# One table of places for all engines' orders, down projection and embedding in four parts, one transfer per broadcast row

## Chip, cores and metric

One core of a Trainium2 chip runs one program. The metric is the device time of one execution in microseconds; the median of three runs stands for the kernel. TensorE is PE, VectorE DVE, ScalarE ACT, GpSimd POOL; SyncE, SP, issues the transfers.

## What is computed

A one-layer model over 64 images with text. Each image's 196 patches of 768 numbers are normalized and projected to 192 (`D`), 128 text rows are appended (324 rows, `L`), then two residual blocks follow.

```python
h = concat([layernorm(patches) @ W + b + pos, txt], axis=1)       # 64 x 324 x 192
x = layernorm(h)
B_, C_ = split(x @ W_bc.T + b_bc)                                  # 16 numbers each (N)
delta = softplus((x @ W_1.T + b_1) @ W_d.T + b_d)                  # 64 x 324 x 192
# for each of 16 states n, along the 324 rows i:
#   s[i] = exp(delta[i] * A[n]) * s[i-1] + delta[i] * B_[i, n] * x[i];   y[i] += s[i] * C_[i, n]
h = h + y
x = layernorm(h)
# 128 experts, the best 6 for each row by sigmoid(x @ Wg.T) + e_bias, weights normalized, times 2.5,
# capacity 192 rows an expert; routed = sum of w * (silu(x @ G) * (x @ U)) @ Dn
shared = (silu(x @ Wsg) * (x @ Wsu)) @ Wsd                         # 928 hidden
h = h + routed + shared
```

## The kernel before

The work is in two stages. `phase1` takes the images in 32 pairs and does everything but the routed experts; `phase2` then runs over the 128 experts (gather rows, two projections, scatter-add). The change is in `phase1` alone.

In `phase1` 192 channels of two images are laid on 128 partitions as three blocks of 324 (`[128, 3, L]`, 972 numbers a partition): 128 channels of the one image, 128 of the other, and the remaining 64 of both, one on each half of the partitions. For each of 16 states `n` there are: `fill_b` (SP loads the row of B into `b_wide[n % 2]`; POOL multiplies it with `du` into `state[n % 4]`), `decay` (ACT, exp into one of two PSUM areas), `scan` (DVE, the recurrence), `load_c` and `fill_c` (SP loads C's row; DVE multiplies; POOL adds to `y`). B, C and the step-size row are small results of PE (`bc_values`) that SP stores to `dram_bc` by six transfers and that are then read back, repeated over partitions: `dram_bc` has 2 x 2 x 16 rows (parity of the pair, half, state) of 9 x 324 numbers (B, C, step size). In `fill_b`, `load_c` and `load_s` each half of the partitions, 64, is filled by a transfer of its own from its own row (L437, L443, L461).

The rest of a pair: `load_x`, `emb_a` and `emb` (patch projection and the sums of squares, PE, into the bank `sums`), `emb_stats`, `emb_scale`; `ln1_stats`, `ln1_apply`, `x1_turn` (transposes), `bc_values`, `step_size`, `softplus` (gives `delta` and `du`, semaphore `du_ready`); after the scans `resid`, `ln2_stats`, `ln2_apply`, `x2_turn`, `gate`, `choose`, `weigh`, `count`; then the shared expert as sixteen pieces `up_g` k (PE two matmuls, ACT tanh into `th`, DVE `ag`) and sixteen `up_u` k (PE two matmuls, DVE product into `inter`), with two PSUM areas taken in turn, and three blocks of `down_a` and `down` (8 matmuls for each of two images, PE, into `sums`; DVE adds), and `store_out`.

All five engines' orders are written out by hand. `schedule(engine)` gives every piece a step on each engine that it uses, 32 steps a body; a piece has a lag, the number of bodies after its pair's scans (negative: before). A body runs all pieces sorted by step, each for the pair that its lag says. `run_bodies` writes the first and last bodies out and makes a loop of two bodies a turn of the 26 in the middle. An engine runs its list strictly in order, and waits on semaphores in front of a piece; so a wait holds up all that stands behind it. Pieces that share the PSUM banks `work` and `sums` count their uses (`use_number`) for these waits. SP is such a list as well: a transfer that has to wait for its buffer holds up the transfers behind it. The experts' loads are `w_up` (96 rows) and `w_down` (116 rows of 3,072 B, L944).

Of the kernel before, what the change touches and what calls it, by code (L numbers as in the profile page):

```python
# [15 lines left out]
PATCH, PC = 768, 6  # L16
# [39 lines left out]

def schedule(engine):
    at = []  # L60

    def put(piece, lag, k, **steps):
        if engine in steps:
            at.append((steps[engine], len(at), (piece, lag, k)))

    for n in range(N):

        b, lag = 2 * n - 4, 0
        if b < 0:
            b, lag = b + 32, -1  # L70
        put("fill_b", lag, n, sp=b, pool=b + 3)
        c, lag = 2 * n - 2.3, 0
        if c < 0:
            c, lag = c + 32, -1
        put("load_c", lag, n, sp=c)
        d, lag = (2 * n - 1.5, 0) if n else (30.5, -1)
        put("decay", lag, n, act=d + 0.3)
        put("scan", 0, n, dve=2 * n)
        put("fill_c", 0, n, dve=2 * n + 1.2, pool=2 * n + 2)
    for k in range(3):  # L80
        put("down_a", 3, k, pe=0.1 + 2 * k)
        put("down", 3, k, pe=1.1 + 2 * k, dve=2.1 + 2 * k)
        put("store_out", 3, k, sp=3.6 + 2 * k)
        put("resid", 1, k, pe=4.9 + 1.8 * k, dve=5.7 + 1.8 * k)
        put("x2_turn", 1, k, pe=15.2 + 1.1 * k, act=16.2 + 1.1 * k)
        put("x1_turn", -1, k, pe=18.2 + 1.1 * k, act=19.2 + 1.1 * k)
    put("load_x", -2, 0, sp=1.5)
    put("load_txt", -1, 0, sp=10.2)
    put("ln2_stats", 1, 0, dve=10.3, act=11.3)
    put("ln2_apply", 1, 0, dve=12.3, act=13)  # L90
    put("emb_scale", -1, 0, dve=11.1)
    put("ln1_stats", -1, 0, dve=12.4, act=13.4)
    put("ln1_apply", -1, 0, dve=14.4, act=15.4)
    for k in range(2):
        put("gate", 1, k, pe=22.1 + k, act=23.3 + k)
        put("emb_a", -2, k, pe=8.5 + 6 * k, act=7.5 + 5.2 * k)
        put("emb", -2, k, pe=9.5 + 5.85 * k, act=13.2 + 5.85 * k)
    put("bc_values", -1, 0, pe=21.5, act=22.3, sp=22.9)
    put("load_s", -1, 0, sp=24.1)
    for k in range(2):  # L100
        put("step_size", -1, k, act=26.2 + k)
    put("softplus", -1, 0, act=28.5, dve=29.2)
    for k in range(3):
        put("choose", 2, k, dve=1.3 + k)
    put("weigh", 2, 0, dve=5)
    put("weigh", 2, 1, dve=6)
    put("count", 2, 0, pe=3.2, dve=5.2)
    put("store_mid", 2, 0, sp=6.5)
    put("find_a", 2, 0, dve=7.5)
    put("find", 2, 0, pe=7.6, dve=8.6)  # L110
    put("emb_stats", -2, 0, dve=20.4, act=21.4)
    for k in range(2 * NJ):
        for n, piece in enumerate(("up_g", "up_u")):
            step = 6.6 + 0.8 * (2 * (k // 2 * 2 + n) + k % 2)
            put(piece, 2, k, pe=step, act=step + 0.6, dve=step + 0.8)
    return [piece for _, _, piece in sorted(at)]


SCHEDULE = {engine: schedule(engine) for engine in ("pe", "act", "dve", "pool", "sp")}

# [3 lines left out]
FIRST_BODY, LOOP_FROM, LOOP_TO, LAST_BODY = -2, 3, 29, PAIRS + 2  # L124
# [7 lines left out]
def bank_uses(i):  # L132

    return [sum(BANK.get(kind) == bank for kind, _, _ in pieces("pe", i)) for bank in (WORK, SUMS)]


def use_number(i, before):


    def use(piece, k, ago=0):  # L140
        bank = BANK[piece]
        same = [(x[0], x[2]) for x in pieces("pe", i - ago) if BANK.get(x[0]) == bank]
        return before[bank] - (len(same) if ago else 0) + same.index((piece, k)) + 1
    return use


def run_bodies(eng, engine, body):

    before = [0, 0]
    add = lambda n, times: [b + x * times for b, x in zip(before, n)]  # L150
    for i in range(FIRST_BODY, LOOP_FROM):
        body(Turn.fixed(i), pieces(engine, i), use_number(i, before))
        before = add(bank_uses(i), 1)
    steady = bank_uses(LOOP_FROM)
    with eng.Fori(0, (LOOP_TO - LOOP_FROM) // 2) as r:
        for q in range(2):
            start = Turn.fixed(LOOP_FROM + q)
            so_far = [x + 2 * n * r for x, n in zip(add(steady, q), steady)]
            body(Turn(start.v + 2 * r, start.p, start.h + r), pieces(engine, LOOP_FROM), use_number(LOOP_FROM, so_far))
    before = add(steady, LOOP_TO - LOOP_FROM)  # L160
    for i in range(LOOP_TO, LAST_BODY + 1):
        body(Turn.fixed(i), pieces(engine, i), use_number(i, before))
        before = add(bank_uses(i), 1)
# [200 lines left out]
def phase1(nc, ctx, a, out, dram_x, dram_cnt, dram_bc, ident, found):  # L364
# [54 lines left out]
    def bc_rows(t, half, first, rows):  # L419

        at = (2 * t.p + half) * N + first
        return dram_bc[at:at + rows]

    with nc.Block() as block:

        @block.sync
        def _(sp):
            def body(i, todo, use):
                for kind, lag, k in todo:
                    t = i.plus(-lag)  # L430
                    if kind == "fill_b":
# [4 lines left out]
                        for half in range(2):  # L436
                            sp.dma_start(b.b_wide[k % 2][HI * half:HI * half + HI].rearrange("p a t -> p (a t)"),  # L437
                                         bc_rows(t, half, k, 1)[:, 0:3 * L].broadcast_to([HI, 3 * L])).then_inc(b_loaded[k % 2], 16)
                    elif kind == "load_c":

                        wait(sp, c_used, N * t.v + k - 1)
                        for half in range(2):
                            sp.dma_start(b.c_wide[k % 2][HI * half:HI * half + HI].rearrange("p a t -> p (a t)"),  # L443
                                         bc_rows(t, half, k, 1)[:, 3 * L:6 * L].broadcast_to([HI, 3 * L])).then_inc(c_loaded[k % 2], 16)
                    elif kind == "bc_values":

                        sp.wait_ge(work_free, use(kind, k))
                        wait(sp, c_used, N * (t.v - 1))
                        for image in range(2):
                            rows = b.bcv[N * image:N * image + N]  # L450
                            for half in range(2):
                                to = bc_rows(t, half, 0, N).rearrange("n (c q t) -> n c q t", c=3, q=3)
                                sp.dma_start(to[:, :, image, :], rows).then_inc(bc_stored, 16)
                                if half == image:
                                    sp.dma_start(to[:, :, 2, :], rows).then_inc(bc_stored, 16)
                    elif kind == "load_s":
# [12 lines left out]
                    elif kind == "store_out":  # L469
                        sp.wait_ge(sums_free, use("down", k))  # L470
# [17 lines left out]
        def _(pool):  # L488
            def body(i, todo, use):
                for kind, lag, n in todo:  # L490
                    t = i.plus(-lag)
                    if kind == "fill_b":
# [3 lines left out]
                        pool.wait_ge(b_loaded[n % 2], 32 * (N // 2 * t.v + n // 2 + 1))  # L496
# [16 lines left out]
        def _(act):  # L513
# [7 lines left out]
            def body(i, todo, use):  # L521
                for kind, lag, k in todo:
# [9 lines left out]
                    elif kind == "emb_a":  # L532
# [608 lines left out]
```

## Time and profile before

| | us |
|---|---|
| median of 3 runs (5800.55 to 5816.44) | 5815.71 |
| profiled execution | 5808.81 |
| its span, first to last instruction | 5806.8 |
| PE busy | 4271.5 (74%) |
| DVE busy | 3764.1 (65%) |
| POOL busy | 3097.6 (53%) |
| ACT busy | 2051.7 (35%) |
| mean granted TensorE clock | 0.838 |
| DMA, mean over the span | 144 GB/s |

"Busy" is the time in which an engine has an instruction under way; the DMA share is the mean busy share of sixteen DMA engines. A stretch that is named by two times is counted from the span's start. "Landing" is the time from a transfer's issue to its semaphore.

### The profile page before, as it was taken

What the parts mean: (1) busy time and instruction counts of PE and PEld (TensorE: products, weight loads), DVE (VectorE), ACT (ScalarE), POOL (GpSimd) and SP (SyncE); (2) the same over time, 40 slices, a digit from 0 to 9 for tenths busy, and PEclk for the clock granted to TensorE, in tenths of its full rate; (3) what the DMA queues carried; (4) which work ended last, traced back from release to release, by engine and by line L of the source; (5) the groups of instructions that cost most, each with busy time, mean ns of one, the idle gap of its engine ahead of it and who ended that gap; (6) DMA issues with size and microseconds to landing.
All of it is one profiled execution on the core that took longest, in us unless ns stands there. A gap on an engine that the chain in (4) does not pass through costs nothing. (4 is left out here: it accounts for less than half of the span.)

```text
span 5806.8 us, 71026 instructions
## 1 busy us (share of the span) xinstructions
PE 4271.5 (74%) x19964; PEld 3364.6 (58%) x19964; DVE 3764.1 (65%) x6446; ACT 2051.7 (35%) x3874; POOL 3097.6 (53%) x1769
## 2 busy tenths in 40 slices
PE   3357777777777777777777777777788788778877
PEld 2335555555555555555555555545677777777777
DVE  2778777778878778777777877786333333333333
ACT  2544454444445444454444445543111111111110
POOL 0765555555556555555555555653255555555554
PEclk7578878888878888878888888889888888888888
DMA  3776666666666666666666666663255555555554
GB/s 89 187 170 172 159 149 156 163 153 166 159 149 161 160 161 157 157 149 156 165 159 157 159 150 161 169 156 90 73 126 126 128 123 128 125 120 128 128 126 105
DMA packets 331418, 837.85 MB, mean 144 GB/s; under 512 B 59152, under 2 KB 143572, under 8 KB 331208
## 3 DMA queue, kind: packets, MB, share of 16 engines
q1 hardware_dynamic: 279928, 764.79, 52.7%
q0 software_dynamic: 49152, 69.84, 6.6%
q10 hardware_dynamic: 2128, 1.26, 0.1%
q14 instruction: 182, 1.49, 0.1%
q8 instruction: 28, 0.46, 0.0%
HBM read 761.92 MB, written 73.75 MB: 144 GB/s over the span
## 5 line engine op out<-in xcount | busy, mean ns | idle before, releaser
L508 POOL TENSOR_TENSOR y<-y,state 128x972 f32<-128x972 f32 x448 | 1027.8, 2294 | 1218.2 <-DVE state L633 1215.3
L498 POOL TENSOR_TENSOR state<-du,b_wide 128x972 f32<-128x972 f32 x512 | 1163.5, 2273 | 356.4 <-DMA b_wide<-bc_rows 191.8
L628 DVE TENSOR_TENSOR_SCAN ps<-ps,state 128x972 f32<-128x972 f32 x512 | 1117.8, 2183 | 106.6 <-POOL state L498 60.6
L780 PE MATMUL ps<-x2f,ws_u 128*116 128x324 f32 x1024 | 503.6, 581 | 574.3 <-DVE ag L765 572.8
L1053 PE MATMUL e_ps<-xgt,w_up 96*116 96x192 f32 x4096 | 730.5, 332 | 24.0 <-DVE e_ag L1026 23.9
L795 PE MATMUL ps<-ws_d,inter 116*98 116x192 f32 (+1 forms) x3072 | 604.9, 360 | 153.4 <-DVE h L639 134.1
L530 ACT ACTIVATE ps<-delta,a_neg 128x648 f32<-128x648 f32 x512 | 410.6, 802 | 855.9 <-DVE state L633 787.3
L1053 PEld LDWEIGHTS e_ps<-xgt,w_up 96*116 96x116 f32 x4096 | 677.3, 183 | 28.4 <-DVE e_ag L1026 26.7
L795 PEld LDWEIGHTS ps<-ws_d,inter 116*98 116x98 f32 (+1 forms) x3072 | 554.8, 193 | 207.6 <-DVE h L639 149.8
L780 PEld LDWEIGHTS ps<-x2f,ws_u 128*116 128x116 f32 x1024 | 190.5, 222 | 763.1 <-DVE ag L765 754.4
L633 DVE TENSOR_TENSOR state<-ps,c_wide 128x972 f32<-128x972 f32 x512 | 596.1, 1164 | 27.0 <-DVE ch L730 9.9
L1011 DVE TENSOR_TENSOR passed<-counts,tk 96x648 f32<-96x648 f32 x128 | 106.2, 829 | 760.9 <-DMA counts<-running_counts,row_idx 760.9
L964 POOL DMA_INDIRECT xg<-token_rows,gather_idx x256 | 244.9, 956 | 647.0 <-DVE gather_idx L1022 592.5
L765 DVE SCALAR_TENSOR_TENSOR ag<-th,ps 116x324 f32<-116x324 f32 x512 | 249.3, 488 | 443.7 <-ACT th L607 441.8
L607 ACT ACTIVATE th<-ps 116x324 f32<-116x324 f32 x512 | 217.2, 434 | 857.1 <-PE ps L781 857.0
L780 PE MATMUL ps<-x2f,ws_g 128*116 128x324 f32 x1024 | 424.2, 499 | 115.7 <-DVE inter L771 111.9
L1088 PE MATMUL e_ps<-w_down,e_inter 116*96 116x192 f32 x2048 | 495.6, 413 | 1.0 <-DVE e_inter L1038 1.0
L781 PE MATMUL ps<-x2f,ws_u 128*116 128x324 f32 x1024 | 455.5, 533 | 0.0
L1088 PEld LDWEIGHTS e_ps<-w_down,e_inter 116*96 116x96 f32 x2048 | 432.0, 217 | 32.7 <-DVE e_inter L1038 1.4
L973 POOL DMA_INDIRECT out_rows<-yo,scatter_idx x256 | 370.7, 1448 | 92.3 <-issue 78.0
L781 PE MATMUL ps<-x2f,ws_g 128*116 128x324 f32 x1024 | 391.7, 466 | 0.0
L842 PE MATMUL ps<-w_tok,x_in 128*98 128x194 f32 x1536 | 389.3, 420 | 0.0
(150 smaller groups left out, 6200.3 us busy)
## 6 DMA issues: line engine op xcount, KB each, us to landing
b_wide<-bc_rows SPq DMA_DIRECT2D x1024, 243.0 KB, 4.9
c_wide<-bc_rows SPq DMA_DIRECT2D x1024, 243.0 KB, 4.1
w_up<-in_we_up SPq DMA_DIRECT2D x128, 696.8 KB
w_down<-in_we_down SPq DMA_DIRECT2D x128, 348.0 KB
x_in<-in_x SPq DMA_DIRECT2D x32, 1176.0 KB, 8.0
soft<-bc_rows SPq DMA_DIRECT2D x64, 243.0 KB, 5.8
bc_rows<-bcv SPq DMA_DIRECT2D x192, 60.8 KB, 2.9
running_counts<-cnt SPq DMA_DIRECT2D x32, 324.0 KB, 3.8
```

Of the source, the lines that this page charges most:

```text
L498: nc.gpsimd.tensor_tensor(b.state[n % 4][:], b.du[t.p][:], b.b_wide[n % 2][:], ALU.mult).then_inc(input_ready, 1)
L508: nc.gpsimd.tensor_tensor(y, y, b.state[n % 4][:], ALU.add).then_inc(y_added, 1)
L530: nc.scalar.activation(to[:, 0:2 * L], b.delta[t.p][:, 0:2, :].rearrange("p a t -> p (a t)"), ACT.Exp, scale=b.a_neg[:, 0, k:k + 1])
L628: nc.vector.tensor_tensor_scan(s, s, b.state[k % 4][:].rearrange("p a t -> p (a t)"), 0.0, ALU.mult, ALU.add).then_inc(scan_done, 1)
L633: nc.vector.tensor_tensor(b.state[k % 4][:].rearrange("p a t -> p (a t)"), state_ps[k % 2], b.c_wide[k % 2][:].rearrange("p a t -> p (a t) ...
L780: nc.tensor.matmul(to, weights[:, 0, cols], b.x2f[t.p][:, q, :], start=True, stop=False)
L781: return nc.tensor.matmul(to, weights[:, 1 + q, cols], b.x2f[t.p][:, 2, :], start=False, stop=True)
L795: mm = nc.tensor.matmul(sums[0:ROWS[k], D * q:D * q + D], b.inter[:, j, q, OFF[k]:OFF[k] + ROWS[k]], b.ws_d[:, j, :], start=(j == 0), stop ...
L842: mm = nc.tensor.matmul(sums[0:98, 196 * c:196 * c + D + 2], b.x_in[:, k, f, at], b.w_tok[:, f, :], start=(f == 0), stop=(f == PC - 1))
L973: nc.gpsimd.indirect_dma_start(out, bass.IndirectOffsetOnAxis(ap=scatter_idx[t.p][:, q:q + 1], axis=0), yo[t.p][:, q, :], None, compute_op ...
L1053: mm = nc.tensor.matmul(ps[0:HC, to_bank + f // 2, CAP * (f % 2):CAP * (f % 2) + CAP], w_up[t.p][:, c, first + HC * f:first + HC * f + HC] ...
L1088: mm = nc.tensor.matmul(ps[0:HALF, 4, D * q:D * q + D], inter[:, f // 2, at:at + HALF], w_down[t.p][:, f, :], start=(f == 0), stop=(f == N ...
```

## The change

`PLACES` holds a place for each piece on each of its engines, counted from the pair's first scan; the place modulo 32 is the step and the whole part of place / 32 is the lag. `schedule` sorts by step. So all orders are laid out anew: scans no longer stand two steps apart, pieces may cross the body's end (a lag can differ between a piece's engines), and the first body is one earlier, with `load_x` alone.

`down_a` and `down` become twelve parts of four matmuls (three blocks of four); `emb_a` and `emb` become eight, the squares' sums and the projection apart; ACT's squaring is the piece `square`. The counting of bank uses is written anew (`uses_bank`, `use`). New waits: PE's `gate` for the third `x2_turn`, `bc_values` for the third `x1_turn`, `up_g` 0 for the third `x2_turn`, and SP's `load_c` 0 for `bc_stored`.

`fill_b`, `load_c` and `load_s` issue one transfer each, with a source of the shape `[2, 64, 972]` from `wide_row` and the whole tile, `[128, 972]`, as destination; the waits count 16 in place of 32.

```diff
-        put("fill_b", lag, n, sp=b, pool=b + 3)
...
-        put("scan", 0, n, dve=2 * n)
...
+    "x2_turn": {
+        "pe": (45.55, 45.57, 45.58,),
+        "act": (41.22, 42.43, 45.43,),
+    },
...
+    "emb": {
+        "pe": (-57.71, -57.05, -55.87, -54.78, -50.43, -50.23, -49.69, -49.33,),
+        "act": (-53.71, -41.87,),
+    },
...
+    "up_g": {
+        "pe": (60.06, 62.7, 72.75, 73.21, 75.69, 77.45, 78.19, 80.54, 83.22, 83.41, 85.16, 85.34, 88.14, 88.74, 90.85, 90.88,),
+        "act": (65.15, 66.19, 70.85, 71.33, 74.42, 76.02, 77.86, 79.7, 82.96, 84.42, 85.35, 86.3, 88.8, 89.67, 92.74, 93.38,),
...
+    "up_u": {
+        "pe": (65.54, 70.13, 73.7, 74.62, 77.98, 79.72, 81.29, 81.87, 84.3, 85.06, 86.85, 87.23, 88.83, 89.44, 91.76, 91.92,),
...
+    "decay": {
+        "act": (1.72, 2.3, 2.8, 3.87, 5.26, 5.58, 6.8, 10.47, 12.62, 15.5, 16.05, 17.64, 21.14, 23.64, 24.25, 30.89,),
+    },
...
+    "scan": {
+        "dve": (2.66, 3.64, 4.95, 5.62, 8.76, 9.67, 12.04, 12.71, 12.79, 16, 19.47, 20.41, 25.99, 27.5, 29.37, 32.52,),
+    },
+    "fill_c": {
+        "dve": (3.65, 3.86, 7.14, 8.25, 10.45, 11.74, 12.09, 13.8, 14.5, 18.73, 21.22, 23.68, 26.52, 28.99, 30.48, 32.96,),
+        "pool": (-1.22, 1.04, 4.28, 5.56, 6.43, 7.38, 12.63, 17.81, 18.27, 19.57, 20.06, 22.27, 23.17, 25.21, 28.88, 31.48,),
+    },
...
+    "fill_b": {
+        "pool": (-6, -5.14, 0.6, 1.54, 3.84, 5.02, 5.58, 9.59, 10.23, 16.62, 16.94, 18.5, 19.54, 20.76, 21.02, 23.13,),
+        "sp": (-6.22, -5.93, -1.55, -1.52, 0.64, 3.2, 3.25, 7.5, 8.57, 12.98, 14.83, 15.14, 16.77, 19.24, 20.03, 23.75,),
+    },
+    "load_c": {
+        "sp": (-3.69, -1.77, -0.03, 1.32, 6.21, 8.22, 9.77, 12.48, 14.42, 16.17, 16.59, 17.32, 20.24, 22.39, 24.8, 24.86,),
+    },
...
+    at = [(places[k], name, k) for name, on in PLACES.items() for e, places in on.items() if e == engine for k in range(len(places))]
+    at = [(place % STEPS, -1 - i, (name, int(place // STEPS), k)) for i, (place, name, k) in enumerate(at)]
+    return [piece for _, _, piece in sorted(at, key=lambda x: (x[0], -x[1]))]
...
+    def wide_row(t, n, c):
+
+        both = dram_bc[2 * t.p * N:2 * t.p * N + 2 * N].rearrange("(h n) (c f) -> n c h f", h=2, c=3)
+        return both[n, c].unsqueeze(1).broadcast_to([2, HI, 3 * L])
...
-                        for half in range(2):
-                            sp.dma_start(b.b_wide[k % 2][HI * half:HI * half + HI].rearrange("p a t -> p (a t)"),
-                                         bc_rows(t, half, k, 1)[:, 0:3 * L].broadcast_to([HI, 3 * L])).then_inc(b_loaded[k % 2], 16)
+                        sp.dma_start(halves(b.b_wide[k % 2]), wide_row(t, k, 0)).then_inc(b_loaded[k % 2], 16)
...
+                        if k == 0:
+                            sp.wait_ge(bc_stored, 96 * t.v + 96)
                         wait(sp, c_used, N * t.v + k - 1)
-                        for half in range(2):
-                            sp.dma_start(b.c_wide[k % 2][HI * half:HI * half + HI].rearrange("p a t -> p (a t)"),
-                                         bc_rows(t, half, k, 1)[:, 3 * L:6 * L].broadcast_to([HI, 3 * L])).then_inc(c_loaded[k % 2], 16)
+                        sp.dma_start(halves(b.c_wide[k % 2]), wide_row(t, k, 1)).then_inc(c_loaded[k % 2], 16)
...
-                        for half in range(2):
-                            sp.dma_start(b.soft[HI * half:HI * half + HI].rearrange("p a t -> p (a t)"),
-                                         bc_rows(t, half, 0, 1)[:, 6 * L:9 * L].broadcast_to([HI, 3 * L])).then_inc(s_loaded, 16)
+                        sp.dma_start(halves(b.soft), wide_row(t, 0, 2)).then_inc(s_loaded, 16)
...
+                    if kind == "down":
+                        part, k = k % 4, k // 4
+                        if part == 0:
+                            pe.wait_ge(inter_ready, 2 * NJ * (t.v + 1))
+                        q, first = part // 2, NJ // 2 * (part % 2)
+                        for j in range(first, first + NJ // 2):
```

## Rows read from the trace of the kernel before

**Rows 1.** The page, parts 2 and 3: 40 slices in tenths, and packet counts.

```profile
DVE  2778777778878778777777877786333333333333
DMA  3776666666666666666666666663255555555554
DMA packets 331418, 837.85 MB, mean 144 GB/s; under 512 B 59152, under 2 KB 143572, under 8 KB 331208
```

**Rows 2.** Windows: two bodies, all scans, the stage's tail, the experts.

```profile
core 0: us, PE busy (x) PEld busy (x) DVE busy (x) ACT busy (x) POOL busy (x), PEclk, DMA share, GB/s
...
2919.80:3041.80 122.00, 89.12 (x361) 62.45 (x359) 97.77 (x152) 58.25 (x109) 67.02 (x30) 0.80 0.62 153
3041.80:3169.20 127.40, 96.33 (x409) 69.98 (x410) 97.61 (x153) 58.15 (x109) 73.41 (x33) 0.85 0.65 161
131.20:3984.50 3853.30, 2771.39 (x11447) 1973.78 (x11447) 3052.57 (x4666) 1811.28 (x3384) 2239.97 (x990) 0.82 0.65 160
3984.50:4127.00 142.50, 129.20 (x606) 96.05 (x606) 65.22 (x170) 23.58 (x55) 2.24 (x1) 1.00 0.07 22
4127.00:5806.80 1679.80, 1326.41 (x7680) 1255.81 (x7680) 620.62 (x1538) 182.56 (x384) 851.90 (x769) 0.87 0.54 123
```

**Rows 3.** Waits of the whole span: waiter <- releaser: us in total, times, longest.

```profile
POOL y L508 <- DVE state L633: 1215.3, 360, 9.8
ACT th L607 <- PE ps L781: 857.0, 252, 23.1
...
PE ps L780 <- DVE ag L765: 572.8, 242, 7.1
DVE ag L765 <- ACT th L607: 441.8, 206, 6.0
...
POOL state L498 <- DMA b_wide<-bc_rows: 191.8, 133, 4.6
```

**Rows 4.** DMA issues: count, KB each, median us from issue to landing.

```profile
b_wide<-bc_rows SPq DMA_DIRECT2D x1024, 243.0 KB, 4.9
c_wide<-bc_rows SPq DMA_DIRECT2D x1024, 243.0 KB, 4.1
...
bc_rows<-bcv SPq DMA_DIRECT2D x192, 60.8 KB, 2.9
```

**Rows 5.** Windows: a stretch in which B and C loads run.

```profile
1441.50:1443.50 2.00, 2.00 (x14) 2.00 (x13) 2.00 (x2) 0.00 (x0) 2.00 (x2) 1.00 0.93 228
```

**Rows 6.** Timeline of SP: start, us, transfer; the first broadcast load, and a later one.

```profile
115.25 1.12 SPq L461 DMA_DIRECT2D soft<-bc_rows  x2
...
1433.23 1.16 SPq L437 DMA_DIRECT2D b_wide<-bc_rows  x2
```

**Rows 7.** Windows: two stretches of the experts with `w_down` alone in flight.

```profile
4289.50:4290.70 1.20, 0.77 (x10) 0.68 (x8) 1.09 (x4) 0.17 (x1) 0.00 (x0) 1.00 0.25 102
...
4143.20:4145.20 2.00, 0.00 (x0) 0.00 (x0) 0.00 (x0) 0.00 (x0) 1.11 (x2) 0.50 0.26 103
```

**Rows 8.** Timeline of SP: the issues around the first of these stretches.

```profile
4287.23 0.26 SPq L944 DMA_DIRECT2D w_down<-in_we_down  x1
4289.85 0.32 SPq L941 DMA_DIRECT2D w_up<-in_we_up  x1
```

**Rows 9.** Groups by line and form: busy us, mean ns of one | idle before.

```profile
L498 POOL TENSOR_TENSOR state<-du,b_wide 128x972 f32<-128x972 f32 x512 | 1163.5, 2273 | 356.4 <-DMA b_wide<-bc_rows 191.8 <-DVE delta L705 163.5
L628 DVE TENSOR_TENSOR_SCAN ps<-ps,state 128x972 f32<-128x972 f32 x512 | 1117.8, 2183 | 106.6 <-POOL state L498 60.6 <-issue 23.7 <-ACT ps L531 13.4
...
L564 ACT ACTIVATE xm<-h,stat 128x64 f32<-128x64 f32 x384 | 164.7, 429 | 156.8 <-DVE stat L698 156.8
...
L565 ACT ACTIVATE x<-h,stat 128x192 f32<-128x192 f32 x192 | 102.4, 533 | 0.0
```

**Rows 10.** Timeline of PE: start, us, instruction, idle before it.

```profile
1453.32 0.71 PE L780 MATMUL ps<-x2f,ws_g 128*116 128x324 f32 x2
...
1458.64 1.43 PE L780 MATMUL ps<-x2f,ws_u 128*116 128x324 f32 x2 [4.07 <-DVE ag L765]
```

More of the change, by code:

```diff
@@ L53, in wait @@
         eng.wait_ge(sem, value)
-def schedule(engine):
[L60 to L70, printed above, removed]
-        put("fill_b", lag, n, sp=b, pool=b + 3)
[L72 to L77, printed above, removed]
-        put("scan", 0, n, dve=2 * n)
[L79 to L116, printed above, removed]
@@ L123, with uses_bank, use @@
         "down": SUMS, "emb": SUMS}
-FIRST_BODY, LOOP_FROM, LOOP_TO, LAST_BODY = -2, 3, 29, PAIRS + 2
+LAST_PART = 3
+def uses_bank(piece, k):
+    return piece in BANK and (k % (LAST_PART + 1) == LAST_PART if BANK[piece] == SUMS else True)
+def use(piece, k, t):
+    mine = next((lag, at) for at, (p, lag, j) in enumerate(SCHEDULE["pe"]) if (p, j) == (piece, k))
+    total = 0
+    for at, (p, lag, j) in enumerate(SCHEDULE["pe"]):
+        if uses_bank(p, j) and BANK[p] == BANK[piece]:
+            first = PAIRS - 1 if p == "find" else 0
+            upto = t.v + (mine[0] - lag) + (0 if at <= mine[1] else -1)
+            if isinstance(upto, int):
+                total = total + max(0, min(upto, PAIRS - 1) - first + 1)
+            elif first == 0:
+                total = total + (upto + 1)
+    return total
 def pieces(engine, i):
     return [x for x in SCHEDULE[engine] if (PAIRS - 1 if x[0] in ("find_a", "find") else 0) <= i - x[1] < PAIRS]
[L132 to L144, printed above, removed]
 def run_bodies(eng, engine, body):
-    before = [0, 0]
-    add = lambda n, times: [b + x * times for b, x in zip(before, n)]
     for i in range(FIRST_BODY, LOOP_FROM):
-        body(Turn.fixed(i), pieces(engine, i), use_number(i, before))
-        before = add(bank_uses(i), 1)
-    steady = bank_uses(LOOP_FROM)
+        body(Turn.fixed(i), pieces(engine, i))
     with eng.Fori(0, (LOOP_TO - LOOP_FROM) // 2) as r:
@@ L157, in run_bodies @@
             start = Turn.fixed(LOOP_FROM + q)
-            so_far = [x + 2 * n * r for x, n in zip(add(steady, q), steady)]
-            body(Turn(start.v + 2 * r, start.p, start.h + r), pieces(engine, LOOP_FROM), use_number(LOOP_FROM, so_far))
-    before = add(steady, LOOP_TO - LOOP_FROM)
+            body(Turn(start.v + 2 * r, start.p, start.h + r), pieces(engine, LOOP_FROM))
     for i in range(LOOP_TO, LAST_BODY + 1):
-        body(Turn.fixed(i), pieces(engine, i), use_number(i, before))
-        before = add(bank_uses(i), 1)
+        body(Turn.fixed(i), pieces(engine, i))
 def build(nc, a, out):
@@ L427, in _, with body @@
         def _(sp):
-            def body(i, todo, use):
+            def body(i, todo):
                 for kind, lag, k in todo:
@@ L488, in _, with body @@
         def _(pool):
-            def body(i, todo, use):
+            def body(i, todo):
                 for kind, lag, n in todo:
@@ L598, in body @@
                     elif kind == "gate":
[L599 removed]
+                        act.wait_ge(work_full, use(kind, k, t))
                         if k == 0:
@@ L619, in newton, with body @@
                 return s[:, 3, :]
-            def body(i, todo, use):
+            def body(i, todo):
                 for kind, lag, k in todo:
@@ L781, in up, with body @@
                 return nc.tensor.matmul(to, weights[:, 1 + q, cols], b.x2f[t.p][:, 2, :], start=False, stop=True)
-            def body(i, todo, use):
+            def body(i, todo):
                 for kind, lag, k in todo:
@@ L787, in body @@
                     if BANK.get(kind) == WORK:
-                        wait(pe, work_free, use(kind, k) - 1)
-                    elif kind in ("down_a", "emb_a"):
-                        wait(pe, sums_free, use(kind[:-2], k) - 1)
-                    if kind in ("down_a", "down"):
-                        pe.wait_ge(inter_ready, 2 * NJ * (t.v + 1))
-                        q = 0 if kind == "down_a" else 1
-                        for j in range(NJ):
+                        wait(pe, work_free, use(kind, k, t) - 1)
+                    elif BANK.get(kind) == SUMS and k % 4 == 0:
+                        wait(pe, sums_free, use(kind, k + 3, t) - 1)
+                    if kind == "down":
[4 more added lines that the diff above has]
+                        for j in range(first, first + NJ // 2):
                             mm = nc.tensor.matmul(sums[0:ROWS[k], D * q:D * q + D], b.inter[:, j, q, OFF[k]:OFF[k] + ROWS[k]], b.ws_d[:, j, :],
                                                   start=(j == 0), stop=(j == NJ - 1))
-                        if q == 1:
+                        if part == 3:
                             mm.then_inc(sums_full, 1)
@@ L813, in body @@
                     elif kind == "gate":
+                        pe.wait_ge(work_free, use("x2_turn", 2, t))
                         for c in range(3):
@@ L850, in body @@
                     elif kind == "up_g":
+                        if k == 0:
+                            pe.wait_ge(work_free, use("x2_turn", 2, t))
                         wait(pe, inter_ready, 2 * NJ * t.v + k - 1)
```

174 lines of the change are left out of this document (139 added, 35 removed).

## Prediction, made before the changed kernel ran

> **What bounds the kernel now.** I read the page first: it has two parts, a long first stage with DVE near eight tenths and DMA at six, and an experts' stage with DVE at three, whose code the diff leaves alone [rows 1]. Then the windows by body: two bodies of the steady loop take 127.4 and 122.0 us, 124.7 on average, with DVE busy 97.7, PE 92.7 at a mean granted clock of 0.82, POOL 70.2, ACT 58.2, and the DMA engines at a share of 0.62 to 0.65 and 153 to 161 GB/s [rows 2]. So no engine is full; DVE has 27 us of idle time in a body. The waits say who causes it: DVE waits for ACT's `th`, ACT for PE's up projection, PE for DVE's `ag`, a ring in which each engine's written-out order makes the next one late; POOL's long wait for `state` costs nothing, as POOL has 54 us to spare. Transfers are hardly in it: POOL waits 191.8 us in all for `b_wide`, 6 us a body, on an engine that is not the bound [rows 3]. The profiled run took 5,808.8 us (span 5,806.8, and 2.0 around it), 0.1% below the median of 5,815.7; I work against the profiled run.
>
> **One transfer per broadcast row.** This is the part that decides. Now each of B, C and the step-size row is brought by two transfers of 64 rows, 243 KB each, of which the B and C ones land 4.9 and 4.1 us after their issue [rows 4]; 66 of them a body. While they run, the DMA share is 0.93 at 228 GB/s: all sixteen engines work [rows 5]. The change issues 33 of twice the size. On SP that saves 33 issues; SP hands out two of them in 1.16 us [rows 6], so some 18 us a body of an engine that no chain needs: worth nothing. What it does to the spread over the engines is the question. The trace has one transfer that is not spread over all sixteen: `w_down`, 116 rows of 3,072 B. In a stretch in which nothing else is in flight (issued at 4287.23, the next issue at 4289.85) the share is 0.25 and the rate 102 GB/s; in another 0.26 and 103 GB/s [rows 7, 8]. A quarter of sixteen is four engines, 25.5 GB/s each, and 4 is the largest number up to 16 that divides 116; 64 rows have 16. So a transfer is cut into equal shares of its outermost count. The new source is `[2, 64, 972]`: two blocks, one for each image's row, with a stride between them, each repeated 64 times with a stride of zero; the two cannot be merged into one count of 128 as the destination's partitions can. If the source's outermost count takes part in the cut, 2 is all that divides it, and each transfer runs on two engines.
>
> The trace of before has no transfer with an outermost count of 2, so the cost has two ends. If the destination's 128 decides, it is sixteen engines and no loss. If the source's 2 decides, each engine carries half of 486 KB, 248,832 B, which at 25.5 GB/s is 9.76 us; all 33 use the same pair if the choice of engines is fixed, one after another: 33 x 9.76 = 322 us a body. Beside them the body moves 19.6 MB (the mean of 161 GB/s x 127.4 us and 153 x 122.0) less 66 x 249 KB = 16.4 MB, so 3.2 MB, spread over sixteen: 0.2 MB on each of the pair, 8 us. I take the second end, 330 us a body, since the only uneven transfer in the trace obeys a divisor and both sides of a copy must be cut alike.
>
> The Trainium skill (DMA: Bandwidth & Descriptors, "Why a DMA increments its semaphore by 16 and not by 1") says that the number of engines is the largest up to 16 that divides the slowest dimension of both access patterns, the lowest-numbered ones being used. By that rule the new transfers have two engines, and `w_down` has four; on `w_down` the trace agrees (0.25 of sixteen), on a count of two no run here shows it.
>
> Is the pair kept busy? SP runs in order, and each B load waits for the fill two before it, each C load for the product two before it. In the new SP order two to four transfers are issued and not landed at nearly every point (c1, b2, b3, c2, b4, c3 of a pair, for example, each wait only for work on rows that have landed). The thin place is `load_s`: it waits until the six stores of `bc_values` have landed, with one C load (9.8 us) queued over it, against a store's 2.9 us [rows 4]. So I add nothing, and let one microsecond between transfers stand as the upper end, 33 us a body.
>
> **The new orders, and the parts of four.** The matmuls, activations and vector instructions are the same in number; `down` and `emb` are only cut where other pieces may stand between. With sixteen engines the bound would be DVE's 97.7 us a body plus what it still waits. I walked the new orders with the mean durations of their groups (the longest and those named below: [rows 9]) from DVE's first piece at no idle time: POOL's fills 3, 5, 7, 8 and 11 end 1 to 3 us before the scans that need them, and POOL's stop at `fill_b` 0 for `softplus`, late in DVE's body, lies before scan 0's place. Two places come late: the twelve activations of `ln2_apply` take 6 x (0.43 + 0.53) = 5.8 us and stand ahead of `x2_turn` 0, `emb` 0, `up_g` 4, `x2_turn` 1 and `decay` 7, so scan 7 waits some 2 us; and `up_u` 4 stands on PE behind three turns and two parts of `emb`, some 4 us late. With two more for what the walk doesn't see (SBUF port waits, the clock) that is 106 us a body. With 330 us a body all of it, and the new waits (`gate` for the third `x2_turn`, `bc_values` for the third `x1_turn`, `up_g` 0, `load_c` 0 for `bc_stored`), is hidden: every compute engine then idles for more than 230 us a body, and they cost nothing. If that cover is gone they are in the 106. The extra body at the front holds only `load_x`: nothing.
>
> **Sum.** Up to the first broadcast load 115.3 us [rows 6]; 32 pairs x 330 = 10,560; from the last scan to the end of the first stage 142.5; experts 1,679.8 [rows 2]; around the span 2.0. Together **12,500 us**, against 5,808.8: the gain of 32 x 19 us in the orders cannot show.
>
> **Rivals.**
> 1. *Sixteen engines*, the other side. The destination's 128 partitions decide, or the two blocks are written out so that sixteen shares come out. Then the DMA engines have the same bytes as before; at 228 GB/s [rows 5] 19.6 MB are 86 us, below DVE's 98. The orders decide: 29 steady bodies x (124.7 - 106) = 542 us less, 5,265 us; 5,150 to 5,500 for stalls of 4 to 16 us a body. For it: the 64-row sources have a stride of zero in their outermost count now and are spread all the same. Against it: that count is 64, not 2. It decides from the point where a transfer has eight or more engines (2.4 us each, 81 us a body).
> 2. *Sixteen engines, but PE becomes the bound.* PE's work of a body is 92.7 us x 0.82 = 76 us at the full 2.4 GHz; in the new order it stands idle for some 6 us between `up_u` 1 and `emb` 0, which waits for the third `down` on DVE, and the granted clock falls to 0.5 (1.2 GHz) in pauses as it does now: two instructions of an up projection take 1.43 us behind a pause of 4.07 us, and 0.71 before it [rows 10]. It costs time once the mean clock is below 76 / 124.7 = 0.61; at 0.58 the body is 131 us, +6 x 32, 6,010 us. Against it: the new order packs PE more tightly.
> 3. *No change*: sixteen engines, and the orders' gain is eaten: 5,809 us.
>
> **How the numbers follow.** Two engines: 0.85, 12,500 us. Sixteen and better orders: 0.11, 5,265. Sixteen and PE-bound: 0.03, 6,010. No change: 0.01. The forecast is the first. Its range: the low end has no other bytes on the pair and a share of 0.245 that the row rounds to 0.25 (26.0 GB/s, 9.57 us): 32 x 316 + 1,939.6 = 12,050, taken as 11,950; the high end has one microsecond lost per transfer: 12,500 + 32 x 33 = 13,560, taken as 13,500. That leaves the 0.15 of the other cases out and some 0.04 of the first. A difference under 0.3% can't be told from none; faster by more 0.11, within it 0.01, slower by more 0.88.
>
> **What would show it.** Right: scans of a pair spread over 330 us; DMA share near 0.13 and some 59 GB/s in the first stage where it is 0.65 and 160 now; the broadcast loads landing 10 us or far more after their issue; POOL waiting for `b_wide` and DVE for `c_wide` as the largest waits; bodies of equal length; DVE busy still 98 us a body; the experts' stage unchanged at 1,680. The skill's same section has each engine used write one semaphore update; if the packets under 512 B count those, they fall from 59,152 [rows 1] by 31,680 with two engines and by 16,896 with sixteen. Wrong: a share of 0.7 or more, `b_wide` landing in 5 us: then rivals 1 to 3, told apart by the body's length. A share near 0.13 with bodies well over 363 us would mean that the pair starves, and the step on the queue is wrong; bodies under 310 us, that an engine alone is faster than 25.5 GB/s.

## The result, and the profile after

The changed kernel takes 12,413.5 us (median of 4; 12,403.1 to 12,422.7) where the kernel before took 5,809.5 beside it: 2.137 times the time, 95% interval 2.133 to 2.141. The forecast was 12,500 us, its range 11,950 to 13,500. The profiled execution took 12,403.1 us.

The page after, parts 1 to 3, beside [rows 1]:

```profile
PE 4684.6 (38%) x19964; PEld 3663.2 (30%) x19964; DVE 3524.7 (28%) x6446; ACT 2077.2 (17%) x3872; POOL 3054.1 (25%) x1769
...
DVE  1222222222222222222222222222222222333333
DMA  1111111111111111111111111111111111255555
...
DMA packets 299845, 839.49 MB, mean 68 GB/s; under 512 B 27472, under 2 KB 111892, under 8 KB 299528
```

The bytes are the same (839 MB against 838), the first stage is stretched over 35 of 40 slices, and in it no engine is busy for more than a third of the time, nor, by its mean, is DMA. Packets under 512 B fell from 59,152 to 27,472, by 31,680: the number forecast for two engines.

Windows after: two bodies, all scans, the tail, the experts, and last two short stretches of a body; columns as in [rows 2].

```profile
5052.20:5379.70 327.50, 110.13 (x408) 79.36 (x406) 90.13 (x152) 59.20 (x109) 68.83 (x31) 0.64 0.16 60
5379.70:5708.20 328.50, 99.51 (x357) 70.40 (x358) 90.01 (x153) 59.06 (x109) 68.90 (x31) 0.63 0.16 60
139.60:10595.90 10456.30, 3183.84 (x11464) 2271.75 (x11465) 2817.67 (x4677) 1841.02 (x3384) 2198.77 (x990) 0.62 0.16 59
10595.90:10738.00 142.10, 128.49 (x591) 95.38 (x589) 59.00 (x159) 23.45 (x54) 2.25 (x1) 0.98 0.08 23
10738.00:12401.00 1663.00, 1329.21 (x7680) 1258.39 (x7680) 622.33 (x1537) 180.94 (x384) 849.75 (x769) 0.87 0.54 124
...
5163.00:5167.00 4.00, 2.69 (x5) 1.28 (x6) 3.79 (x14) 2.95 (x4) 0.37 (x1) 0.50 0.13 52
5172.00:5176.00 4.00, 0.00 (x0) 0.00 (x0) 0.00 (x0) 0.36 (x1) 0.00 (x0) 0.50 0.13 50
```

A body takes 328 us, long and short ones alike. The last two rows are what to look at: while only broadcast rows are in flight the share is 0.13, two of sixteen engines, and the rate 50 to 52 GB/s, 25 to 26 an engine; in the second of them PE, DVE and POOL do nothing at all.

Waits of the whole span, beside [rows 3]:

```profile
POOL state L575 <- DMA b_wide<-bc_rows: 7050.7, 475, 126.2
DVE state L710 <- DMA c_wide<-bc_rows: 6026.7, 485, 25.5
```

POOL waited 191.8 us for `b_wide` before and waits 7,050.7 now; DVE waits 6,026.7 for `c_wide`. The next longest wait, 5,310.9 us of ACT, is for DVE's product with `c_wide`.

### The profile page after: what moved, and what is told of

Its sections match the earlier page's. It is cut to its first block and busy times, and to the rows that moved or that the text cites. A ratio compares the mean times of both kernels' runs of the same rounds, so it can differ in the third digit from the quotient of the medians.

```text
span 12401.3 us, 70269 instructions
## 1 busy us (share of the span) xinstructions
PE 4684.6 (38%) x19964; PEld 3663.2 (30%) x19964; DVE 3524.7 (28%) x6446; ACT 2077.2 (17%) x3872; POOL 3054.1 (25%) x1769
## 2 busy tenths in 40 slices
DMA packets 299845, 839.49 MB, mean 68 GB/s; under 512 B 27472, under 2 KB 111892, under 8 KB 299528
## 5 line engine op out<-in xcount | busy, mean ns | idle before, releaser
L575 POOL TENSOR_TENSOR state<-du,b_wide 128x972 f32<-128x972 f32 x512 | 1144.9, 2236 | 7164.8 <-DMA b_wide<-bc_rows 7050.7
L710 DVE TENSOR_TENSOR state<-ps,c_wide 128x972 f32<-128x972 f32 x512 | 599.1, 1170 | 6029.9 <-DMA c_wide<-bc_rows 6026.7
L857 PE MATMUL ps<-x2f,ws_u 128*116 128x324 f32 x1024 | 571.2, 653 | 2564.0 <-DVE ag L842 2564.0
L857 PE MATMUL ps<-x2f,ws_g 128*116 128x324 f32 x1024 | 572.2, 654 | 2068.4 <-DVE inter L848 2068.4
L607 ACT ACTIVATE ps<-delta,a_neg 128x648 f32<-128x648 f32 x512 | 411.5, 804 | 5333.2 <-DVE state L710 5310.9
L585 POOL TENSOR_TENSOR y<-y,state 128x972 f32<-128x972 f32 x448 | 999.0, 2230 | 1221.0 <-DVE state L710 1209.1
L857 PEld LDWEIGHTS ps<-x2f,ws_u 128*116 128x116 f32 x1024 | 230.9, 257 | 2745.2 <-DVE ag L842 2686.4
L857 PEld LDWEIGHTS ps<-x2f,ws_g 128*116 128x116 f32 x1024 | 251.8, 270 | 2223.6 <-DVE inter L848 2128.2
L874 PEld LDWEIGHTS ps<-ws_d,inter 116*98 116x98 f32 (+1 forms) x3072 | 587.3, 202 | 984.5 <-DVE h L716 882.3
L858 PE MATMUL ps<-x2f,ws_u 128*116 128x324 f32 x1024 | 518.7, 600 | 0.0
L858 PE MATMUL ps<-x2f,ws_g 128*116 128x324 f32 x1024 | 507.2, 587 | 0.0
L881 PE MATMUL ps<-ident,y 128*98 128x128 f32 (+1 forms) x288 | 83.2, 425 | 929.1 <-DVE h L729 562.4
L921 PE MATMUL ps<-ones,x_sq 128*98 128x2 f32 x1536 | 209.6, 264 | 488.1 <-DVE h L716 324.7
```

What stands on the lines that cost most here:

```text
L575: nc.gpsimd.tensor_tensor(b.state[n % 4][:], b.du[t.p][:], b.b_wide[n % 2][:], ALU.mult).then_inc(input_ready, 1)
L585: nc.gpsimd.tensor_tensor(y, y, b.state[n % 4][:], ALU.add).then_inc(y_added, 1)
L607: nc.scalar.activation(to[:, 0:2 * L], b.delta[t.p][:, 0:2, :].rearrange("p a t -> p (a t)"), ACT.Exp, scale=b.a_neg[:, 0, k:k + 1])
L710: nc.vector.tensor_tensor(b.state[k % 4][:].rearrange("p a t -> p (a t)"), state_ps[k % 2], b.c_wide[k % 2][:].rearrange("p a t -> p (a t) ...
L857: nc.tensor.matmul(to, weights[:, 0, cols], b.x2f[t.p][:, q, :], start=True, stop=False)
L858: return nc.tensor.matmul(to, weights[:, 1 + q, cols], b.x2f[t.p][:, 2, :], start=False, stop=True)
```

## Experiments

Five questions: is it the transfer or the order; is it the number of engines; does the rule of divisors hold; what are the new orders worth without the loss; and where does the time come from that one transfer in place of two saves. Each ratio is to the kernel before, run beside it; its median there was between 5,772 and 5,810 us, so compare ratios rather than times. `after_rows_in_turn`, `before_rows_in_turn`, `before_one_row` and `before_two_in_turn` put rows on other partitions than the computation needs, and serve for timing alone.

### The one part undone, and done alone

`after_two_transfers`, in each of the three loads:

```diff
-                        sp.dma_start(halves(b.b_wide[k % 2]), wide_row(t, k, 0)).then_inc(b_loaded[k % 2], 16)
+                        for half in range(2):
+                            sp.dma_start(b.b_wide[k % 2][HI * half:HI * half + HI].rearrange("p a t -> p (a t)"), half_row(t, k, 0, half)).then_inc(b_loaded[k % 2], 16)
```

> The changed kernel with one part undone: each broadcast row is again brought by two transfers of 64 rows, one for each half of the partitions; orders and parts of four stay as changed. Theory A (each transfer of two blocks runs on two DMA engines, and these are the whole loss): the DMA share of the scans' stage is back above 0.65, a body takes about 106 us, 5,265 us in all, 5,150 to 5,500. Rival B (the new orders keep SP's transfers waiting, and the shape of the transfer costs nothing): still about 12,400 us, share 0.13. Rival C (sixteen engines, but PE becomes the bound in the new orders): about 6,000 us.

Measured: 5,203.9 us, ratio 0.9032 (0.8987 to 0.9078).

`before_one_transfer` makes the opposite edit in the kernel before, with `wide_row` and `halves` as in the change.

> The kernel before with this one part of the change: one transfer a row with a source of two blocks of 64, the old orders. Theory A: 33 x 9.54 us on the two engines and some 8 us of other traffic, the same 328 us a body as the changed kernel, 12,400 us within 1%, whatever the order. Rival B: within 2% of 5,810 us. If the old order keeps fewer transfers queued than the new one, the body is longer than 328 us by the gaps, up to 33 us.

Measured: 12,378.4 us, ratio 2.148 (2.141 to 2.155). Two bodies of the first and two of the second, in the windows view:

```profile
1882.10:1988.00 105.90, 82.71 (x385) 61.98 (x385) 91.36 (x154) 59.05 (x109) 67.62 (x31) 0.92 0.75 185
1988.00:2093.50 105.50, 81.42 (x384) 59.77 (x383) 92.20 (x153) 58.87 (x109) 70.84 (x32) 0.92 0.75 188
```

```profile
5053.30:5710.00 656.70, 225.19 (x766) 153.82 (x766) 180.99 (x305) 118.56 (x218) 137.36 (x63) 0.62 0.16 60
```

The loss goes with the one transfer into the old orders (656.7 / 2 = 328.4 us a body, as after the change) and leaves the new ones when it is undone. (33 x 9.54 + 8, as it stands in the expectation, is 323; 328 takes 9.7 us a row.) Rival B falls twice, and no gap shows in the old order either. What is left is the gain of the new orders with their parts of four: 105.7 us a body against 124.7 [rows 2], 9.7% of the whole.

### The number of engines

`after_rows_in_turn` and `before_rows_in_turn` change one thing in `wide_row`, in the changed kernel and in `before_one_transfer`:

```diff
-        return both[n, c].unsqueeze(1).broadcast_to([2, HI, 3 * L])
+        return both[n, c].unsqueeze(0).broadcast_to([HI, 2, 3 * L])
```

> The changed kernel with the two dimensions of the source exchanged: 64 repeats outside, the two images' rows inside, so still one transfer of the same 486 KB from the same two rows. Part of the computation is changed: partition 2r gets the row of the first image and 2r + 1 that of the second, where the halves should have them. Theory A: the outermost counts are 64 and 128, sixteen engines, 5,265 us as with two transfers, less at most what 33 issues of 0.55 us on SP are worth. Rival D (one transfer of both rows is slow in itself, by its size or by reading two rows over and over, not by the number of engines): about 12,400 us.

> The kernel before with one transfer a row, source of 64 repeats outside and two rows inside (same change of the computation: the two images' rows alternate over partitions). Theory A: sixteen engines, so only the 33 issues saved on SP are left of this part: 5,810 us less 0 to 3% (POOL waits 6 us a body for b_wide now, and the row lands some 0.5 us earlier). Rival D: about 12,400 us.

Measured: 5,162.7 us, ratio 0.8958 (0.8928 to 0.8989), and 5,664.9 us, ratio 0.9833 (0.980 to 0.9866). One transfer of 486 KB from the same two rows is not slow; with 64 as the outermost count it is even a little faster than two transfers. The destination is the same `[128, 972]` in both cases, so it is the source's outermost count that decides; `w_down`, with 116 on both sides, could not tell. Rival D falls. Windows of a body of each:

```profile
1956.70:2061.70 105.00, 83.84 (x384) 62.90 (x383) 90.94 (x154) 58.85 (x109) 71.17 (x32) 0.90 0.59 189
```

```profile
1988.60:2109.60 121.00, 93.42 (x412) 68.08 (x413) 97.23 (x153) 58.11 (x109) 73.47 (x33) 0.87 0.53 170
```

Then plain sources, whose row count alone sets the number. `parts_of_62_and_2`, and likewise 57 and 7, on the changed orders:

```diff
+                        for half in range(2):
+                            for at, rows in ((0, 62), (62, 2)):
+                                sp.dma_start(b.b_wide[k % 2][HI * half + at:HI * half + at + rows].rearrange("p a t -> p (a t)"), half_row(t, k, 0, half, rows)).then_inc(b_loaded[k % 2], 16)
```

> The changed kernel's orders, each broadcast row by four plain transfers: of each half's 64 rows one transfer of 62 and one of 2, all with a source of one count (one image's row repeated) and no second block. 62 and 2 are divisible by no number up to 16 above 2. Theory A (the number of engines is the largest up to 16 that divides the outermost count, and nothing else about the source matters): 2 x (31 + 1) = 64 rows on each of two engines, as in the changed kernel, 328 us a body, 12,410 us within 1%, share 0.13. Rival E (the two-block source is what is slow, plain sources are not): 5,200 to 5,500 us.

> The same with 57 and 7 rows of each half: three engines and seven. If the engines are always the lowest-numbered, each of the first three carries 2 x (19 + 1) = 40 rows of a broadcast row; a row took 0.1517 us in the changed kernel ((328.3 - 8) / 33 / 64), so 6.07 us, 33 x 6.07 = 200, and 8 for the other traffic: 208 us a body, 8,560 us in all within 3%, and a DMA share of about 0.20 (16.4 MB and 3.2 MB at 25.6 GB/s an engine in 208 us). If the seven engines of the small transfers are others than the three, 190 + 8 = 198 us a body, 8,240. Rival E: 5,200 to 5,500.

Measured: 12,399.7 us, ratio 2.135 (2.125 to 2.145), and 8,745.7 us, ratio 1.506 (1.499 to 1.513). Windows: two bodies of 62 and 2 in one row, then two bodies of 57 and 7:

```profile
5000.00:5657.00 657.00, 213.64 (x771) 152.68 (x769) 180.28 (x306) 118.17 (x218) 137.69 (x62) 0.64 0.16 60
```

```profile
2041.00:2252.50 211.50, 105.70 (x403) 77.75 (x404) 91.28 (x153) 59.13 (x109) 68.97 (x31) 0.72 0.27 93
2252.50:2465.80 213.30, 96.39 (x365) 69.14 (x363) 91.57 (x153) 59.00 (x109) 68.98 (x31) 0.72 0.27 93
```

Without any second block, rows in a number that only 2 divides give 328.5 us a body again. With 57 = 3 x 19 it is 212.4, against 208 worked out for three engines that also carry their part of the small transfers, and 198 if they don't. So the three engines of the 57 rows are among the seven of the 7 rows, as far as this shows; the 4 us above are not explained, nor is the share of 0.27 where about 0.20 was expected. Rival E falls. By the Trainium skill (DMA: Bandwidth & Descriptors, "Why a DMA increments its semaphore by 16 and not by 1") the counts are 2 and 3; these runs agree, with 328 and 212 us a body.

The small packets count the engines as well. DMA packets of `after_rows_in_turn`, `parts_of_62_and_2` and `parts_of_57_and_7`:

```profile
DMA packets 314629, 839.55 MB, mean 163 GB/s; under 512 B 42256, under 2 KB 126676, under 8 KB 314312
...
DMA packets 306247, 840.05 MB, mean 68 GB/s; under 512 B 33808, under 2 KB 118228, under 8 KB 305864
...
DMA packets 318919, 840.10 MB, mean 96 GB/s; under 512 B 46480, under 2 KB 130900, under 8 KB 318536
```

If each engine of a transfer adds one packet under 512 B, the 2,112 transfers of 64 rows before make 33,792 of the 59,152 [rows 1] and leave 25,360 for all else. To these come 1,056 x 16, 2,112 x (2 + 2) and 2,112 x (3 + 7), which gives the three counts exactly, and 1,056 x 2 gives the 27,472 after the change.

### What the new orders hold

`decay_9_earlier`, on `after_two_transfers`. A body of that kernel, timeline of DVE, shows where it waits:

```profile
1894.65 0.55 DVE L724 TENSOR_TENSOR h<-h,ps 98x384 f32<-98x384 f32 x1 [5.04 <-PE ps L882]
...
1929.73 2.18 DVE L713 TENSOR_TENSOR_SCAN ps<-ps,state 128x972 f32<-128x972 f32 x1
1934.26 0.49 DVE L856 TENSOR_TENSOR inter<-ag,ps 116x324 f32<-116x324 f32 x1 [2.35 <-PE ps L866]
...
1945.19 2.19 DVE L713 TENSOR_TENSOR_SCAN ps<-ps,state 128x972 f32<-128x972 f32 x1 [1.80 <-ACT ps L616]
```

These are the second `down` block, scan 7 with no wait, `up_u` 4, and scan 9.

```diff
-        "act": (1.72, 2.3, 2.8, 3.87, 5.26, 5.58, 6.8, 10.47, 12.62, 15.5, 16.05, 17.64, 21.14, 23.64, 24.25, 30.89,),
+        "act": (1.72, 2.3, 2.8, 3.87, 5.26, 5.58, 6.8, 10.47, 12.62, 14.8, 16.05, 17.64, 21.14, 23.64, 24.25, 30.89,),
```

> The changed orders with two transfers a row, and ACT's decay 9 at 14.8 in place of 15.5, so ahead of the twelve activations of ln1_apply. In the run with two transfers the scan of state 9 is the one that waits for ACT, 1.64 us a body. If that wait is on the path, 1 to 1.6 us less a body, 5,150 to 5,175 against 5,204; if ACT is then late for x1_turn and bc_values by the same 1.3 us, no change.

Measured: 5,307.4 us, ratio 0.9149 (0.9112 to 0.9185): 1.3% slower than without the edit. DVE's waits for ACT, first of `after_two_transfers`, then of this run:

```profile
DVE ps L713 <- ACT ps L616: 65.8, 57, 4.8
...
DVE ag L850 <- ACT th L692: 43.6, 39, 5.4
```

```profile
DVE ag L850 <- ACT th L692: 154.6, 61, 5.4
...
DVE ps L713 <- ACT ps L616: 19.3, 27, 5.2
```

The wait of the scans went, 46 us, as meant; 111 us came up at `ag`. A body of this run shows how, in the timelines of ACT, PE and DVE (the second line of PE was 0.71 us in the body of `after_two_transfers`):

```profile
1974.19 0.81 ACT L615 ACTIVATE ps<-delta,a_neg 128x648 f32<-128x648 f32 x1 [3.01 <-DVE state L718]
...
1979.92 0.77 PE L898 MATMUL ps<-ident,xn 98*128 98x98 f32 x3 [3.96 <-ACT xn L650]
1980.49 1.29 PE L865 MATMUL ps<-x2f,ws_g 128*116 128x324 f32 x2
...
1982.89 0.44 ACT L692 ACTIVATE th<-ps 116x324 f32<-116x324 f32 x1 [3.12 <-PE ps L866]
...
1983.37 0.49 DVE L850 SCALAR_TENSOR_TENSOR ag<-th,ps 116x324 f32<-116x324 f32 x1 [4.38 <-ACT th L692]
```

Decay 9 now stands ahead of `ln1_apply` and waits 3.01 us for the PSUM area that `fill_c` 7 frees; `ln1_apply` starts 2.3 us after its statistics are there, PE waits 3.96 us for its result and then runs its next products at half the pace (the granted clock is 0.50 from 1980.0 to 1983.3, and was 1.00 over the same pieces in `after_two_transfers`), and `up_g` 7 behind them is late for DVE. Neither outcome that I had written down allowed a loss.

`emb_in_blocks`, on `after_two_transfers`:

```diff
-        "pe": (-57.71, -57.05, -55.87, -54.78, -50.43, -50.23, -49.69, -49.33,),
+        "pe": (-57.71, -57.7, -57.69, -57.68, -50.43, -50.42, -50.41, -50.4,),
```

> The changed orders with two transfers a row, the four parts of each emb block put one behind the other on PE, at the place of the first (-57.71 and -50.43), so the cut into parts is undone for the embedding in its effect. The parts of down stand together in the table already. If the parts are worth something, it is here: 6.2 us of emb at the full clock then stand ahead of resid 1 and 2 and up_g 2, and of x2_turn 2 and up_u 4; the part of it that DVE has no other work for is lost, 2 to 6 us a body, 5,270 to 5,400 us. If the parts do nothing: 5,204 within 0.5%.

Measured: 5,439.8 us, ratio 0.9371 (0.9336 to 0.9406). The ratios differ by 0.034, some 200 us or 6 us a body, at the upper end of what was expected (the time itself lies above the 5,400 written down). In the waits of this run

```profile
DVE h L735 <- PE ps L889: 137.1, 29, 7.6
DVE inter L856 <- PE ps L866: 170.4, 168, 3.2
```

the first, `resid`, was not among the sixty longest before (its transposes now stand behind the whole block), and the second was 105.9. So a third of the orders' gain is lost when the embedding's parts stand in one block at the place of the first; a block at another place was not tried. Those of `down` follow each other in the table within a block; there the cut changes no order.

### One transfer in place of two

The rows in turn had been faster than two transfers by 1.7% in the old orders, where I had put nothing. Either 33 issues fewer on SP, or the two rows read in turn. `before_one_row` and `before_two_in_turn` are `before_one_transfer` with

```diff
+        return both[n, c, 0:1].broadcast_to([128, 3 * L])
```

```diff
+        return both[n, c].unsqueeze(0).broadcast_to([HI // 2, 2, 3 * L])
```

the second for each half, by a transfer of its own.

> The kernel before, one transfer of 128 rows for each broadcast row, all 128 from the first image's row (so part of the computation is changed: the second image's half has the first one's row). Sixteen engines, 33 issues a body as in the run with the two rows in turn, but one source row for all engines as before. That run was 1.7% faster than before, and its packets of 3,888 B took 152 ns in the median where before took 261. Theory F (the time comes from the 33 issues saved on SP): ratio 0.983 here too. Theory G (it comes from the rows in turn, which let packets pass faster): ratio 1.00 and a DMA share of 0.62 to 0.65 as before.

> The kernel before with its two transfers of 64 rows a broadcast row, each taking the two images' rows in turn (32 repeats outside, two rows inside; the rows then alternate over the partitions, which changes part of the computation). 66 issues as before, packets from two rows. Theory F: ratio 1.00. Theory G: ratio 0.983 and a DMA share near 0.50.

Measured: 5,700.1 us, ratio 0.9829 (0.9809 to 0.9849), and 5,779.4 us, ratio 0.9965 (0.9951 to 0.9978). The times are those of theory F: one transfer in place of two gives 1.7%, the rows in turn 0.35%. The waits of `before_one_row` show where: POOL's for `b_wide` is halved, from 191.8 [rows 3] to

```profile
POOL state L500 <- DMA b_wide<-bc_rows: 92.7, 67, 2.8
```

Theory G's share went the other way round as well. In a stretch of 600 us, `before_one_row` and then `before_two_in_turn`:

```profile
1900.00:2500.00 600.00, 456.79 (x1931) 327.60 (x1932) 489.51 (x764) 291.20 (x546) 354.65 (x157) 0.84 0.53 165
```

```profile
1900.00:2500.00 600.00, 453.32 (x1864) 324.84 (x1863) 476.32 (x749) 280.35 (x525) 337.22 (x150) 0.82 0.64 157
```

More bytes a microsecond at a lower share: the low share belongs to one transfer of 128 rows, not to which rows it reads. So `before_one_row` changes two things, SP's issues and the form of the transfer, and no run parts them. The landings speak for the issues: a transfer of 128 rows lands 4.8 us (`b_wide`) and 3.7 us (`c_wide`) after its issue, one of 64 rows 4.9 and 4.1 [rows 4], and the second of two is issued some 0.6 us after the first [rows 6].

`after_two_copies` reads two copies in turn, on `after_two_transfers`:

```diff
+        copies = dram_bc.rearrange("(w r) (c f) -> r c w f", w=2, c=3)[(2 * t.p + half) * N + n, c]
+        return copies.unsqueeze(0).broadcast_to([HI // 2, 2, 3 * L])
...
-                            for half in range(2):
-                                to = bc_rows(t, half)
+                            for half, copy in ((0, 0), (0, 1), (1, 0), (1, 1)):
+                                to = bc_rows(t, half, copy)
```

> The changed orders with two transfers of 64 rows, and two copies of every B, C and step-size row in DRAM, read in turn (32 repeats outside, two copies inside); twelve stores in place of six. Nothing of the computation is changed. By theory G the packets take less, the share falls from 0.75 to about 0.6 and the time goes to about 5,160 to 5,190 us, below the 5,204 of the run with two transfers; the six stores more cost 3.7 us of SP a body and put load_s as much later, which DVE's softplus has room for. By theory F it is 5,204 or some us more.

Measured: 5,338.2 us, ratio 0.9213 (0.920 to 0.9227), 2.0% slower than `after_two_transfers`. It gains nothing from the turn (in 600 us of the steady loop the share is 0.76, against 0.75), which fits F, but it loses more than F allowed. SP's six stores more stand in front of loads, and `b_wide` is waited for 592.5 us against 466.3 there; that this is the cause was not tested.

```profile
POOL state L583 <- DMA b_wide<-bc_rows: 592.5, 183, 10.8
```

Of the kernels that compute all of it, `after_two_transfers` is the fastest, below the kernel before and the changed one. One transfer with sixteen engines and the halves where they belong was not tried.

## Why the prediction was right, point by point

- **The bound, before.** A ring of waits among DVE, ACT and PE, no full engine. The new orders take 9.7% off with the same number of instructions on PE, DVE and POOL, so it was the order. That it was this ring is argued and not shown; its waits in `after_two_transfers` fit, with DVE's for ACT at 43.6 us (441.8 before) and PE's for DVE at 282.9 (572.8 before):

```profile
ACT th L692 <- PE ps L866: 520.9, 292, 15.7
...
PE ps L865 <- DVE ag L850: 282.9, 200, 5.3
```

- **Two engines.** Inferred from `w_down`'s quarter [rows 7], which showed a divisor but not whose: that the source's count takes part was an assumption, which nothing in the trace of before tested. Two engines are shown by the share of 0.13 in clean stretches, by the 31,680 small packets, by both swaps of the one part, by the rows in turn, and by 62 and 57 rows.
- **The price.** 9.76 us a broadcast row and 8 for the rest of the traffic, 330 us a body; measured 328.3, which is 9.71 us a row if the 8 stand. The profiled run lies 97 us below the sum: 32 x 1.7 = 54 us are that, 17 us the experts' stage (1,663 against 1,679.8), and some 25 us the ends, where shorter pairs (322.5 us the first, 298.6 the last, in place of 330) outweigh a first scan 24 us after the 115.3 from which the sum counted.
- **No starving.** I added nothing for gaps. Bodies are equal to 1 us after the change, and as long in the old orders; 9.7 us a row is what the clean stretches give as well (248,832 B at 25 to 26 GB/s), so nothing shows that the pair of engines starved.
- **All else hidden.** The two kernels with two engines and different orders differ by 0.3% (12,413 and 12,378).
- **DVE busy "still 98 us" was wrong:** it is 90. Groups by line of DVE, before and after:

```profile
L704 DVE TENSOR_TENSOR du<-delta,xf 128x972 f32<-128x972 f32 x32 | 93.0, 2907 | 1.1
L748 DVE SCALAR_TENSOR_TENSOR block_of<-slot,cnt,block_of 128x192 f32<-128x192 f32 x64 | 102.1, 1596 | 1.1
```

```profile
L781 DVE TENSOR_TENSOR du<-delta,xf 128x972 f32<-128x972 f32 x32 | 37.5, 1171 | 1.1
L825 DVE SCALAR_TENSOR_TENSOR block_of<-slot,cnt,block_of 128x192 f32<-128x192 f32 x64 | 26.5, 413 | 1.1
```

  The product `du` took 2.9 us and takes 1.17, `block_of` 1.6 and 0.41: together 4.1 of the 7.5 us a body, the rest in small instructions. In the bodies looked at, POOL had a product under way beside both before and none after. It is the place that counts, not a POOL that idles in the mean: in `after_two_transfers`, with POOL as busy as before in each body, both stand in pauses of POOL and take 1.29 and 0.49 us in the mean. I had summed busy time as if it were work.
- **The share "near 0.13"** was that of clean stretches; the body's is 0.16. I had left the other traffic out: 8 us on each of sixteen engines in 328 are another 0.024, which makes 0.15; the last 0.01 is not explained.
- **A sign that can't be read:** that the broadcast loads land 10 us or far more after their issue. The page after gives no landing for them.
- **The term sized wrongly: "33 issues fewer on SP: worth nothing".** One transfer in place of two is worth 1.7% in the old orders and 0.8% in the new ones (0.9032 to 0.8958, the rows in turn included), when the engines stay sixteen. SP has time to spare, but each second transfer is issued half a microsecond late, in front of a POOL that waits for it; how much is the issue and how much the form of the transfer is open, as said above. Here it was buried under the loss.
- **Rival 1, the orders with sixteen engines:** 5,265 us worked out, 5,204 measured, in its range; 106 us a body against 105.7. Most of the difference is not the orders': the experts' stage, whose code is the same, took 1,630 us in that run (1,679.8 before), which is not explained. The size of the body was right by luck in part: of the two places, `up_u` 4 was late (2.35 us in the body shown, 4 worked out) but scan 7 was not; scan 9 was, and `down` 1, which I had not seen. And 6 us a body came as shorter DVE work (97.7 to 91.8), which the walk had not.

## What to carry to other kernels

Look at the outermost count of both sides of a transfer before joining two into one: a count of 2 in front put all of it on two of sixteen DMA engines, and a part of the change that looked like a saving of issues cost more than the whole kernel had taken. The sign in a trace is a low DMA share while engines wait for DMA; in a short stretch with a single kind of transfer in flight it stands at a small multiple of a sixteenth, which gives the number of engines and the rate of one. The count of small packets gives it too. Test a change of many parts by undoing one: the same diff held a gain of 9.7%.

## What the runs showed of the hardware

- One DMA engine moved 25 to 26 GB/s with rows of 3,072 B (four engines, [rows 7]) or 3,888 B (two, 50 to 52 GB/s together); with three, 204 us for 33 x 40 rows of 3,888 B on each make 25. Sixteen at once gave 228 GB/s at a share of 0.93 [rows 5], 15 each.
- SP's issues grew long. Timeline of SP after the change:

```profile
5153.12 0.53 SPq L517 DMA_DIRECT2D b_wide<-bc_rows  x1
5153.70 5.92 SPq L523 DMA_DIRECT2D c_wide<-bc_rows  x1
5159.73 9.01 SPq L517 DMA_DIRECT2D b_wide<-bc_rows  x1
5168.79 10.04 SPq L523 DMA_DIRECT2D c_wide<-bc_rows  x1
5179.05 9.12 SPq L545 DMA_DIRECT2D h<-in_txt  x1
```

  A single issue took from 0.53 us to 10, often near the 9.7 us of one broadcast row, even for the small text load. It looks as if an issue waits for room on the two engines; no run tested it.
- The DMA share is not a measure of load: 165 GB/s at 0.53 with one transfer of 128 rows, 157 at 0.64 with two of 64. Why packets stand longer with two is open.
